# A graph layer's constants and two second parts of adjacency pieces made on GpSimd, with the copy of tile 1 and the split of piece 0 moved

## The reference: what is computed

```python
h = jnp.maximum(_layernorm(x), 0.0)
# layer 0: 4-bit activations, 3-bit weight
w_norm = (weight - mean(weight)) / std(weight, ddof=1)
weight_q = round(|clip(w_norm / wgt_alpha)| * 7) * sign(w_norm)    # in steps
x_q = round(minimum(h / act_alpha, 1) * 15)                        # in steps
support = relu(x_q @ weight_q * act_delta * wgt_delta)
support_q = round(minimum(support / act_alpha2, 1) * 15)
x = x + (adj / scale) @ support_q * scale * act_alpha2 / 15
# layer 1: attention whose aggregator matrix is adj
h = jnp.maximum(_layernorm(x), 0.0)
x = x + mean over heads of softmax(where(adj == 1, scores, -inf), diagonal 1e-07) @ h
```

## Time and profile before

| | us |
|---|---|
| median of 3 runs | 152.7 (152.53 to 153.63) |
| profiled execution, its own time | 152.72 |
| its span in the profile | 150.9 |
| busy: PE, DVE, ACT, POOL | 137.2, 108.8, 103.8, 33.2 |

### The profile page before, as it was taken

The page is one execution under the profiler, slowest core; times in us unless marked ns, Lnnn a source line. Parts: engine busy times, 40 slices in busy tenths (PEclk is TensorE's granted clock), DMA queues, the critical chain, the costliest instruction groups (busy, mean ns, idle before and its releaser), DMA issues.

```text
span 150.9 us, 2112 instructions
## 1 busy us (share of the span) xinstructions
PE 137.2 (91%) x686; PEld 86.3 (57%) x686; DVE 108.8 (72%) x230; ACT 103.8 (69%) x154; POOL 33.2 (22%) x64
## 2 busy tenths in 40 slices
PE   0398999999999999999999999999999999999920
PEld 0384545556455555657574747575666657579920
DVE  0888887999866459996862696776968797765451
ACT  3578947688778679605964999999999788511000
POOL 2352144242230000016010201101010742711010
PEclk9999999999999999999999999999999999999997
DMA  5999999613131690260179899999111021011102
GB/s 150 320 411 418 401 398 415 276 37 70 35 76 35 178 413 0 26 256 0 17 249 416 235 378 369 367 356 354 45 72 69 0 74 69 0 69 69 69 9 72
DMA packets 11837, 27.44 MB, mean 182 GB/s; under 512 B 5040, under 2 KB 5296, under 8 KB 9776
## 3 DMA queue, kind: packets, MB, share of 16 engines
q1 hardware_dynamic: 11536, 26.88, 50.4%
q10 hardware_dynamic: 288, 0.39, 0.9%
HBM read 22.03 MB, written 4.19 MB: 174 GB/s over the span
## 4 chain that ended last, share of the span: by engine, by line
PE 81%; issue 5%; DMA 3%; DVE 3%; POOL 2%; ACT 1%; SPq 1%; POOLq 0%; DVEq 0%
PE acc L1048 27%; PE acc L1044 25%; PE acc L1028 9%; PE acc L1023 9%; PE acc L1010 8%; DMA w_sb<-weight 3%; PE acc L1056 2%; PE acc L996 2%; POOL rs L569 1%; SPq L308 1%; ACT h_i L431 1%; DVE ring L829 1%; DVE x_sb L953 1%; DVE st L756 0%; DVE w_st L834 0%
## 5 line engine op out<-in xcount | busy, mean ns | idle before, releaser
L1048 PE MATMUL acc<-sup,lo 128*128 128x512 f32 (+1 forms) x208 | 48.3, 384 | 0.0
L1044 PE MATMUL acc<-sup_h,hi 128*128 128x512 f16 (+1 forms) x208 | 43.7, 363 | 0.0
L1048 PEld LDWEIGHTS acc<-sup,lo 128*128 128x128 f32 x208 | 37.0, 188 | 7.9
L554 POOL TENSOR_SCALAR nm<-mv 128x1 f32<-128x1 f32 (+2 forms) x19 | 12.9, 676 | 99.1 <-DVE ve L766 78.6
L412 ACT ACTIVATE junk<-raw,below 128x2048 uint8<-128x2048 f32 x16 | 31.8, 1988 | 0.0
L1044 PEld LDWEIGHTS acc<-sup_h,hi 128*128 128x128 f16 x208 | 19.4, 98 | 21.4 <-issue 2.9
L811 DVE TENSOR_TENSOR lo<-raw,hi 128x2048 fp32r<-128x2048 f32 x11 | 25.2, 2288 | 7.5 <-ACT hi L404 7.5
L446 ACT ACTIVATE ring<-x_sb,nm 128x512 f32<-128x512 f32 x15 | 10.4, 715 | 20.4 <-POOL nm L554 17.1
L1028 PE MATMUL acc<-sup,lo 128*128 128x512 f32 x64 | 22.2, 453 | 0.1
L404 ACT ACTIVATE hi<-raw 128x2048 f16<-128x2048 f32 x11 | 20.9, 1896 | 0.0
L756 DVE BATCH_NORM_STATS2 st<-x_sb 128x6 f32<-128x512 f32 x29 | 19.5, 688 | 0.4
(11 more groups left out here) (76 smaller groups left out, 83.2 us busy)
## 6 DMA issues: line engine op xcount, KB each, us to landing
raw<-adj_t SPq DMA_DIRECT2D x16, 1024.0 KB, 6.6
out<-ring SPq DMA_DIRECT2D x15, 256.0 KB, 5.6
x_sb<-x SPq DMA_DIRECT2D x3, 1024.0 KB, 14.1
w_sb<-weight SPq DMA_DIRECT2D x4, 258.0 KB, 4.0
x_sb<-x SPq DMA_DIRECT2D x1, 512.0 KB, 6.1
x_sb<-x ACTq DMA_DIRECT2D x1, 256.0 KB, 3.7
x_sb<-x SPq DMA_DIRECT2D x1, 256.0 KB, 5.2
h_iT<-h_i SPq DMA_TRANSPOSE x8, 2.4
```

Of the source, the lines that this page charges most:

```text
L1044: nc.tensor.matmul(bank[:, cols], part(hi, k % PARTS, j), sup_h[:, j, cols], start=(j == 0), stop=False)
L1048: ins = nc.tensor.matmul(bank[:, cols], part(lo, k % PARTS, j), sup[:, j, cols], start=False, stop=(j == T - 1))
```

## The change

GpSimd makes seven one-column constants that VectorE made. It also makes the second part (`lo`) of pieces 0 and 2 (`lo_of_piece` in its own stream), in an order with the small operations that is written out. VectorE copies tile 1's transpose with its bounds (`bound_hT(1)`) instead of ScalarE. ScalarE splits piece 0 ahead of `relu_sup(0)`. On VectorE the variance of tiles 2 and 3 comes after the support of tile 0, and that of tiles 4 and 5 before the copy of tile 2's transpose. There are 18 warm-up matmuls instead of 20 after tile 0's transposes. The semaphores follow: consumers of a `lo` piece wait for `lo_by_pool` for pieces 0 and 2, and for `lo_piece` otherwise.

```diff
--- before.py
+++ after.py
@@ -51,7 +51,7 @@
     TURN = 8
     SLOTS = 4
 
-    WARM_SUMS, WARM_FIRST, WARM_T = 16, 4, (20, 0)
+    WARM_SUMS, WARM_FIRST, WARM_T = 16, 4, (18, 0)
     RAW = 7
     PARTS = 3
     RING = 4
@@ -168,7 +168,9 @@
         w_rounded = sem("w_rounded")
         wq_ready = sem("wq_ready")
         qin_ready = sem("qin_ready")
+        const_part = sem("const_part")
         consts_ready = sem("consts_ready")
+        const_out = sem("const_out")
         x_summed = sem("x_summed")
         x_mean = sem("x_mean")
         x_squared = sem("x_squared")
@@ -189,6 +191,7 @@
         sup_ready = sem("sup_ready")
         sup_h_ready = sem("sup_h_ready")
         hi_piece = sem("hi_piece")
+        lo_by_pool = sem("lo_by_pool")
         lo_piece = sem("lo_piece")
         hi_ready = sem("hi_ready")
         lo_ready = sem("lo_ready")
@@ -251,10 +254,17 @@
                 eng.wait_ge(h_ready, j - EARLY + 1)
 
         def wait_hT(eng, j):
-            if j < EARLY:
-                eng.wait_ge(hqT_ready, j + 1)
+            if j == 0:
+                eng.wait_ge(hqT_ready, 1)
             else:
-                eng.wait_ge(hqT_bounded, j - EARLY + 1)
+                eng.wait_ge(hqT_bounded, j)
+
+        def wait_lo_piece(eng, p):
+
+            if p in (0, 2):
+                eng.wait_ge(lo_by_pool, p // 2 + 1)
+            else:
+                eng.wait_ge(lo_piece, 1 if p == 1 else p - 1)
 
 
         def wait_hi(eng, k):
@@ -265,7 +275,9 @@
 
         def wait_lo(eng, k):
             if k <= GT:
-                eng.wait_ge(lo_piece, 4 * (k + 1))
+                wait_lo_piece(eng, 4 * k + 3)
+                if k == 0:
+                    eng.wait_ge(lo_by_pool, 2)
             else:
                 eng.wait_ge(lo_ready, k - GT)
 
@@ -469,9 +481,8 @@
             act.wait_ge(w_bias, 1)
             round_w(2)
             round_w(3)
-            copy_T(1)
+            split_piece(0)
             relu_sup(0)
-            split_piece(0)
             relu_sup(1)
             split_piece(1)
             round_h(2)
@@ -568,15 +579,39 @@
             def inverse_root(a, m):
                 nc.gpsimd.tensor_tensor(rs[:, a:a + m], ve[:, a:a + m], minus_half[:, 0:m], ALU.pow).then_inc(r_ready, 1)
 
+            def cc(i):
+                return cn[:, i:i + 1]
+
+            def scs(i):
+                return w_sb[:, 0, D + i:D + i + 1]
+
+            def lo_of_piece(p):
+                pool.wait_ge(hi_piece, p + 1)
+                cols = slice(p * PIECE, (p + 1) * PIECE)
+                nc.gpsimd.tensor_tensor(lo[:, 0, cols], raw[:, 0, cols], hi[:, 0, cols],
+                                        ALU.subtract).then_inc(lo_by_pool, 1)
+
+
+            pool.wait_ge(w_in[0], 16)
+            nc.gpsimd.tensor_scalar(cc(C_IQ), scs(S_AA), 1.0 / ACT_LEVELS, None, ALU.mult).then_inc(const_part, 1)
+            nc.gpsimd.tensor_scalar(cc(C_SUP0), scs(S_AA), 1.0 / WGT_LEVELS, scs(S_WA), ALU.mult,
+                                    ALU.mult).then_inc(const_part, 1)
+            pool.wait_ge(const_part, 1)
+            nc.gpsimd.tensor_tensor(cc(C_IQ2), cc(C_IQ), cc(C_IQ), ALU.mult).then_inc(consts_ready, 1)
             pool.wait_ge(half_ready, 1)
             mean_of_sum(0)
             var_of_squares(0)
             inverse_root(0, 1)
+
+            nc.gpsimd.tensor_scalar(cc(C_W), cc(C_RWA), WGT_LEVELS, None, ALU.mult).then_inc(consts_ready, 1)
+            pool.wait_ge(const_part, 2)
+            nc.gpsimd.tensor_tensor(cc(C_SUP), cc(C_SUP0), cc(C_RAA2), ALU.mult).then_inc(consts_ready, 1)
             mean_of_sum(1)
             pool.wait_ge(w_var, 1)
             nc.gpsimd.tensor_tensor(ws(W_ROOT), ws(W_VAR), minus_half[:, 0:1], ALU.pow).then_inc(w_root, 1)
             var_of_squares(1)
             inverse_root(1, 1)
+            lo_of_piece(0)
             for n in range(EARLY + 1, FIRST + 1):
                 a, m = first_ln[n - 1]
                 centre(n, a, m)
@@ -585,6 +620,12 @@
                 pool.wait_ge(nm_ready, n)
                 pool.wait_ge(r_ready, n)
                 nc.gpsimd.tensor_tensor(nb[:, a:a + m], nm[:, a:a + m], rs[:, a:a + m], ALU.mult).then_inc(nb_ready, 1)
+                if n == EARLY + 1:
+                    lo_of_piece(2)
+            nc.gpsimd.tensor_tensor(cc(C_OUT0), cc(C_RSC), scs(S_SCALE), ALU.mult).then_inc(const_part, 1)
+            pool.wait_ge(const_part, 3)
+            nc.gpsimd.tensor_scalar(cc(C_OUT), cc(C_OUT0), 1.0 / ACT_LEVELS, scs(S_AA2), ALU.mult,
+                                    ALU.mult).then_inc(const_out, 1)
             for s in range(GT, T):
                 n = FIRST + 1 + s - GT
                 centre(n, *second_ln[s - GT])
@@ -736,16 +777,6 @@
                 dve.wait_ge(w_in[0], 16)
                 chain(nc.vector.reciprocal(cn[:, C_RSC:C_RAA2 + 1], w_sb[:, 0, D:D + 4]))
                 nc.vector.tensor_scalar(cc(C_QIN), cc(C_RAA), ACT_LEVELS, None, ALU.mult).then_inc(qin_ready, 1)
-                nc.vector.tensor_scalar(cc(C_IQ), scs(S_AA), 1.0 / ACT_LEVELS, None, ALU.mult)
-
-            def constants():
-                nc.vector.tensor_scalar(cc(C_W), cc(C_RWA), WGT_LEVELS, None, ALU.mult)
-                nc.vector.scalar_tensor_tensor(cc(C_SUP0), scs(S_AA), 1.0 / WGT_LEVELS, scs(S_WA), ALU.mult, ALU.mult)
-                nc.vector.tensor_tensor(cc(C_IQ2), cc(C_IQ), cc(C_IQ), ALU.mult)
-                chain(nc.vector.tensor_tensor(cc(C_OUT0), cc(C_RSC), scs(S_SCALE), ALU.mult))
-                nc.vector.tensor_tensor(cc(C_SUP), cc(C_SUP0), cc(C_RAA2), ALU.mult)
-                nc.vector.scalar_tensor_tensor(cc(C_OUT), cc(C_OUT0), 1.0 / ACT_LEVELS, scs(S_AA2), ALU.mult,
-                                               ALU.mult).then_inc(consts_ready, 1)
 
             def wait_x(t):
                 for n, (a, m) in enumerate(x_loads):
@@ -790,8 +821,9 @@
                 else:
                     dve.wait_ge(h_turned[j % 2], 16 * ((j - TURN) // 2 + 1))
                     turned = h_iT[:, j % 2, :, :].rearrange("p k i -> p (k i)")
-
-                dve.wait_ge(sup_in_psum, j - 1)
+                if j >= 2:
+
+                    dve.wait_ge(sup_in_psum, j - 1)
                 nc.vector.tensor_scalar(h_qT[:, j % 2, :], turned, 0.0, ACT_LEVELS, ALU.max, ALU.min).then_inc(hqT_bounded, 1)
 
             def quantise_sup(i):
@@ -847,7 +879,6 @@
             first_constants()
             chain(w_stats(1))
             nc.vector.bn_aggr(w_half[:, :], w_st[:, 0:KD // 2, :].rearrange("p k s -> p (k s)")).then_inc(w_sum, 1)
-            constants()
             w_stats(2)
             after = step(w_stats(3))
             dve.wait_ge(w_tot, 1)
@@ -868,7 +899,7 @@
             stats(2)
             dve.wait_ge(w_root, 1)
             dve.wait_ge(dve_chain, after)
-            dve.wait_ge(consts_ready, 1)
+            dve.wait_ge(consts_ready, 3)
             W = D * D
             chain(nc.vector.tensor_scalar(ws(W_SCALE), ws(W_ROOT), cc(C_W), ((W - 1.0) / W)**0.5, ALU.mult, ALU.mult))
             nc.vector.scalar_tensor_tensor(ws(W_BIAS), ws(W_SCALE), -1.0, ws(W_MEAN), ALU.mult, ALU.mult).then_inc(w_bias, 1)
@@ -880,18 +911,17 @@
             for k in range(KD // 2, KD):
                 dve.wait_ge(w_rounded, k - KD // 2 + 1)
                 clip_w(k)
-            normalise(3, stats(3))
+            bound_hT(1)
+            last = stats(3)
             quantise_sup(0)
-            lo_of_piece(0)
+            normalise(3, last)
             quantise_sup(1)
+            lo_of_piece(1)
             wait_x(4)
             stats(4)
-            lo_of_piece(1)
-            last = stats(5)
+            normalise(4, stats(5))
             bound_hT(2)
-            normalise(4, last)
             bound_hT(3)
-            lo_of_piece(2)
             quantise_sup(2)
 
 
@@ -944,6 +974,7 @@
                     lo_of_piece(T + 2)
                     lo_of_piece(T + 3)
                     split_lo(GT + 1)
+            dve.wait_ge(const_out, 1)
             for s in range(GT, T + 1):
                 a, m = second_ln[s - GT]
                 sources = ([(t, acc[t % 8], slice(0, D)) for t in range(a, a + m)] if s < T else
@@ -1022,7 +1053,7 @@
                     at = (j % GT) * GT + t
                     nc.tensor.matmul(acc[t][:, :], part(hi, k % PARTS, at), sup_h[:, j, :], start=(j == 0), stop=False)
                 pe.wait_ge(sup_ready, j + 1)
-                pe.wait_ge(lo_piece, j + 1)
+                wait_lo_piece(pe, j)
                 for t in rows:
                     at = (j % GT) * GT + t
                     ins = nc.tensor.matmul(acc[t][:, :], part(lo, k % PARTS, at), sup[:, j, :], start=False, stop=(j == T - 1))
```

## The result

| | us | beside it, before |
|---|---|---|
| median of 19 runs | 153.12 (152.57 to 154.31) | 152.53 (152.08 to 154.26), 19 runs |
| ratio | 1.0044 [1.0024, 1.0064] | |
| profiled execution, its own time | 152.77 | 152.72 |
| its span | 151.0 | 150.9 |

The two profiled executions differ by 0.05 us only, so their spans show nothing of it: the trace has to be read in pieces. The page of the changed kernel first: span and instructions, then busy time, its share of the span and the number of instructions of each engine.

What follows compares the result with a forecast made beforehand. TensorE was taken to bound the kernel from tile 4's transposes on, so delays there reach the end whole. 152.72 us, nothing for weight and warm-ups, -0.36 + 0.36 at the start and +0.7 gave 153.4, range 152.1 to 154.9.

Steps and rivals of the forecast that it cites:

- The weight path gains nothing: Weight statistics on VectorE: the fourth waits for its quarter landing at 7.21 us, so moving the constants is worth 0.
- Warm-ups: TensorE before tile 1's transposes: two warm-up matmuls less, 0.23 us, are worth 0.
- Aggregation starts 0.36 earlier: First aggregation on TensorE: it waits for tile 0's support copy, not piece 0, and starts 0.36 us earlier.
- T(2) waits for h(2): Transposes of tile 2 wait for its rounding behind the moved variance and start at 18.3 us as before; 0.36 lost.
- Piece 2 ahead of pair (4, 5): On GpSimd, a 1.16 us subtraction delays the pair's small operations; transposes of tile 4 start at 23.3 us, +0.7.
- Sum: Whole kernel: 152.72 + 0 (weight) + 0 (warm-up) - 0.36 + 0.36 (start) + 0.7 = 153.4 us.
- Rival 1: VectorE and GpSimd block each other: +2.8 us, 155.5; decides from about 1.6 us per GpSimd subtraction; chance 0.14.
- Rival 2: GpSimd's subtraction takes 0.68 us and its small operations 1.2 us a pair: 152.1 us; chance 0.22.
- Rival 3: Two warm-ups less delay the clock's rise past the support matmuls: up to 1.7 us more, 155 us; chance 0.05.
- That it does nothing: All moved work hides and tile 4's transposes stay at 22.59 us within 0.2: 152.7 us; chance 0.14.
- The signs: In the changed profile, tile 4's transposes at about 23.3 us would mean right, before 22.6 us wrong.

Runs made afterwards that it cites:

- e8: The kernel before, measured once more with no edit: 152.66 us, ratio 1.0028 to the kernel before.
- e3: The changed kernel with the variance of tiles 2 and 3 first again and piece 2's second part back on VectorE: 151.37 us, ratio 0.9922 to the kernel before.
- e7: The changed kernel with 20 warm-up matmuls instead of 18: 152.80 us, ratio 1.0011 to the kernel before.
- e4: The kernel before with only its seven constants moved to GpSimd: 152.09 us, ratio 0.9972 to the kernel before.
- e5: The changed kernel with piece 2's subtraction done twice on GpSimd: 154.14 us, ratio 1.0095 to the kernel before.
- e6: The changed kernel with piece 0's subtraction done twice on GpSimd: 153.90 us, ratio 1.0063 to the kernel before.
- e1: The changed kernel with piece 2's second part back on VectorE: 152.18 us, ratio 0.9964 to the kernel before.

## Why the prediction was nearly right, point by point

The forecast was 153.4 us, +0.7; measured were 153.12 and +0.59, a second time +0.30. The mechanism was the forecast one, T(4) waiting for h(4) through GpSimd. The sum had three errors: the constants (0 forecast, about -0.3 found), T(2) (0, +0.27) and T(2) to T(4) (+0.71, +0.34). The first and third outweigh the second and leave about +0.3, so that +0.59 came so near to +0.7 is in part luck.

- **The weight path gains nothing: this step failed.** I read a fourth statistics that starts as its quarter lands, at 7.21, and took the landing for fixed and the constants for hidden. But the third had started at 6.52, straight behind the constants, and with the quarter there the fourth would have followed about 0.6 behind it, as in e8, where the two took 1.28 us and not 1.41: in that one execution two limits nearly coincided. The landing moves by 1 us from profile to profile (about 6.5 in e3, 7.6 in e7); with an earlier landing the constants were the limit. Taking them away gives up to 0.37 us in the profiles (e4 against e8), some 0.3 in the medians.
- **Warm-ups:** 0 forecast, and nothing seen (e7).
- **Aggregation starts 0.36 earlier:** 0.37 measured, with `sup_h` of tile 0 as its releaser.
- **T(2) waits for h(2):** right, released by `h_i`, but mis-sized. From the end of the variance (14.94) to the end of `nb` (16.99) the pair took 2.05 us, where I took its own 1.72. `z_sup` of tile 1 now follows at once (14.03 instead of 15.05), so VectorE's two copies of it and the subtraction of piece 1 lie beside `nm` and `rs`, which took 0.53 and 1.13 instead of 0.23 and 0.76 before (only `nb` was shorter, 0.20 against 0.54). I had moved that `z_sup` forward myself, two paragraphs earlier, and not asked what it meets. The cost is +0.27 where 0 was forecast. `nm` and `rs` before:

```profile
14.28 0.23 POOL L554 TENSOR_SCALAR nm<-mv 128x2 f32<-128x2 f32 x1 [2.86 <-DVE ve L771]
...
14.47 0.76 POOL L569 TENSOR_TENSOR rs<-ve,minus_half 128x2 f32<-128x2 f32 x1
```

- **Piece 2 ahead of pair (4, 5):** right in place and in price: 1.16 us from 19.23, forecast 1.16 from T(2) + 1.3. The small operations behind took 1.22 us (20.39 to 21.61) instead of 1.6: `nm` fell into VectorE's wait for `z_sup`, and `rs`, begun just before the two copies, kept its 0.73. T(2) to T(4) thus 4.63, not 5.0. The estimate from the Trainium skill (GPSIMD Engine Reference, Elementwise — side-by-side cycle accounting), 1.12 us, was 0.04 short of the trace.
- **Sum:** +0.27 + 0.34 = +0.61 from `z_sup` to T(4), against the 0.71 forecast; less about 0.3 from the constants leaves +0.3. The two measurements, +0.59 and +0.30, lie at and above it; by e8, 0.25 us between equal kernels is within what such a measurement does.
- **Rival 1 (blocking)**: its mechanism is real (e5, e6), but at 1.16 us the operation stays under the point from which it decides. **Rival 2 (a little faster)** needed a subtraction of 0.68 us and small operations of 1.2 us a pair; the subtraction took 1.16, and of the pairs only (4, 5), with 1.22, came out so. What it is worth once the two late steps are undone is e3. **Rival 3 (the clock)**: no cost of the 18 warm-ups was seen (e7), and T(1), after 0.82 us of idle, ran in 0.40 us, no slower than T(2). **That it does nothing** is out by the distance.
- **The signs** were given as absolute times, and these misled: T(4) at 22.52 is under the 22.6 that was to mean "wrong", and within 0.2 of 22.59, which was to mean "it does nothing". The start had moved by 0.68 between the two profiles. A sign counted from `z_sup` would have held.

## What to carry to other kernels

A wait that ends at a landing is one limit, not the limit: look at what the waiting engine did until then, and if it finished within a few tenths, both bind. When an edit brings an operation forward, ask what it now runs beside; two small GpSimd operations took 0.3 and 0.4 us more that way. And a queue in order charges moved work at whoever stands behind it: 1.16 us moved to an engine that is idle three quarters of the time cost 0.6 (e1), because the next pair's mean stood behind it.

## What the runs showed of the hardware

- GpSimd's fp32 less fp16 subtraction of 128x512 took 1.15 or 1.16 us in every profile where it ran free, VectorE's 0.67 to 0.69. A VectorE copy from SBUF to SBUF that starts beside it lasts until it ends (e5: 1.03 us instead of 0.29, e6: 1.38 instead of 0.42), and in e6 the subtraction that began with `sup_h` at 14.41 took 1.30 instead of 1.16, so GpSimd seems to wait as well; `bn_stats` and the copy from PSUM (`h_qT`, 19.03 + 0.42 in the profile after) don't wait.
- TensorE's rise to the full clock falls at another moment from one execution to the next, with the same work ahead of it. e8 and the profile of before are the same kernel: there the 20 warm-ups took 2.34 us and T(1) 0.61, here, in the timeline of e8:

```profile
9.89 1.41 PE L1056 MATMUL acc<-ident 128*128 128x128 bf16 x20
...
12.21 0.40 PE L996 MATMUL acc<-ident,h_i 128*128 128x128 bf16 x4 [0.92 <-DVE h_i L782]
```

  and in the timeline of e7, whose work up to here is that of the change with 20 warm-ups:

```profile
10.41 2.34 PE L1087 MATMUL acc<-ident 128*128 128x128 bf16 x20
...
12.73 0.61 PE L1027 MATMUL acc<-ident,h_i 128*128 128x128 bf16 x4
```

  20 matmuls of 128 columns in 2.34 us is the 1.2 GHz level, 1.41 us mostly the 2.4 GHz one; the granted clock stands at 1.00 in the table of every stretch of both. From T(1) to `z_sup` it took 1.35 us in e8 and after, 1.55 before, 1.93 in e7: 0.6 us of scatter ahead of the distance. What decides the moment no run here shows.
